# Row maxima and row sums of an attention stage moved through DRAM, and score banks seeded by ScalarE in every step

## What is computed

```python
xn = group_norm(x, gn_gamma, gn_beta)
qkv = jnp.einsum('bchw,oc->bohw', xn, w_qkv).reshape(B, 3, nh, d, H * W)   # nh = 4, d = 64
q, k, v = (qkv[:, 0], qkv[:, 1], qkv[:, 2])
scores = jnp.einsum('bhci,bhcj->bhij', q, k) * d ** (-0.5)
attn = jax.nn.softmax(scores, axis=-1)
out = jnp.einsum('bhij,bhcj->bhci', attn, v).reshape(B, C, H, W)
proj = jnp.einsum('bchw,oc->bohw', out, w_proj) + b_proj[None, :, None, None]
return xn + proj
```

## Time and profile before

| what | value |
|---|---|
| median of 3 runs | 5492.59 us (5486.8 to 5498.76) |
| the profiled execution | 5486.11 us |
| its span, from first to last instruction | 5484.3 us |
| PE busy in the span | 4957.6 us (90%) |
| DVE busy | 3959.3 us (72%) |
| POOL busy | 2966.1 us (54%) |
| ACT busy | 2793.4 us (51%) |
| granted PE clock, mean | 0.959 of full speed |

### The profile page before, as it was taken

The page is one execution under the profiler, slowest core; times in us unless marked ns, Lnnn a source line. Parts: engine busy times, 40 slices in busy tenths (PEclk is TensorE's granted clock), DMA queues, the critical chain, the costliest instruction groups (busy, mean ns, idle before and its releaser), DMA issues. The chain is left out here.

```text
span 5484.3 us, 73719 instructions
## 1 busy us (share of the span) xinstructions
PE 4957.6 (90%) x22320; PEld 2313.6 (42%) x22320; DVE 3959.3 (72%) x6354; ACT 2793.4 (51%) x4750; POOL 2966.1 (54%) x2339
## 2 busy tenths in 40 slices
PE   7999999999899999999978869969978996999788
PEld 3333333333333333333346657745544553554344
DVE  4788888883588888888333334458887886898898
ACT  2666666664266666666411111135544554555455
POOL 0555555555055555555437757746645664665675
PEclk9999999999999999999978879989999998999899
DMA  2000000000000000000134435569969998998998
GB/s 73 1 1 1 1 1 1 1 1 34 30 1 1 1 1 1 1 1 1 37 87 128 128 111 163 162 242 365 388 268 350 371 389 304 378 387 350 396 410 358
DMA packets 320271, 812.24 MB, mean 148 GB/s; under 512 B 70094, under 2 KB 137556, under 8 KB 319758
## 3 DMA queue, kind: packets, MB, share of 16 engines
q0 software_dynamic: 193536, 679.59, 32.8%
q1 hardware_dynamic: 126478, 129.39, 6.9%
HBM read 708.40 MB, written 100.43 MB: 147 GB/s over the span
## 5 line engine op out<-in xcount | busy, mean ns | idle before, releaser
L653 POOL TENSOR_TENSOR arena<-arena 128x1024 f32<-128x1024 f32 x480 | 1168.0, 2433 | 955.2 <-ACT arena L1310 952.6
L1841 DVE TENSOR_REDUCE arena<-ps 128x2 f32<-128x1024 f32 x1024 | 1252.2, 1223 | 457.5 <-PE ps L805 454.2
L705 POOL DMA_INDIRECT arena<-corners,arena x1152 | 1094.2, 950 | 687.6 <-issue 301.6
L1310 ACT ACTIVATE arena<-ps 128x1024 f32<-128x1024 f32 x1024 | 995.4, 1022 | 611.2 <-PE ps L834 609.4
L2065 DVE SCALAR_TENSOR_TENSOR ps<-arena,ps 128x256 f32<-128x256 f32 x2304 | 956.3, 483 | 230.9 <-DVEq L2059 220.9
L1172 PE MATMUL ps<-arena 128*128 128x512 f32 x2304 | 1047.5, 598 | 0.2
L834 PE MATMUL ps<-arena 64*128 64x512 f32 x4096 | 977.9, 590 | 19.0 <-ACT ps L1293 19.0
L847 PE MATMUL ps<-arena 128*64 128x512 f32 x4096 | 991.3, 605 | 0.0
L1503 ACT ACTIVATE ps<-arena 128x256 f32<-128x256 f32 x1152 | 500.2, 469 | 471.0 <-DMA arena<-corners,arena 208.4
L689 POOL DMA_INDIRECT arena<-corners,arena x576 | 544.8, 946 | 275.5 <-issue 244.3
L1860 DVE TENSOR_TENSOR arena<-arena 128x1024 f32<-128x1024 f32 x480 | 630.5, 1314 | 79.3 <-ACT arena L1310 79.3
(11 more groups left out here) (165 smaller groups left out, 4108.5 us busy)
## 6 DMA issues: line engine op xcount, KB each, us to landing
corners<-arena SPq DMA_DIRECT2D x256, 256.0 KB
arena<-corners,arena POOLq DMA_INDIRECT x1728, 7.7
img<-in_x SPq DMA_DIRECT2D x8, 1024.0 KB, 9.3
corners<-arena SPq DMA_DIRECT2D x128, 64.0 KB, 2.2
arena<-in_wd SPq DMA_DIRECT2D x2, 2304.0 KB, 8.5
between<-img SPq DMA_DIRECT2D x4, 1024.0 KB, 5.9
arena<-between SPq DMA_DIRECT2D x4, 1024.0 KB, 10.5
resid<-img SPq DMA_DIRECT2D x8, 512.0 KB, 3.4
```

The source lines that it names most:

```text
L653: pool.tensor_tensor(SUMS[u % 2][:, 0], SUMS[u % 2][:, 0], PAIR[g % 2][:, :, 0], ALU.add).then_inc(sum_a, 2)
L705: pool.indirect_dma_start(G3[4 * k + t].rearrange("p a c -> p (a c)"), None, table256[b], bass.IndirectOffsetOnAxis(ap=IS3[:, k, t:t + 1], ...
L1310: af(P[n % 4].rearrange("p h q -> p (h q)"), ps[:, 2 * (n % 2):2 * (n % 2) + 2, :].rearrange("p h q -> p (h q)"), ACT.Exp, scale=float(D) ...
L1841: v.tensor_reduce(mxp[i % 2][:, :, j], ps[:, 4:6, :], AX.X, ALU.max).then_inc(mx_done, 1)
```

## The change

The maxima no longer go through PE and ACT. DVE writes the negated maximum of eight steps to MNEG and scales it into MROWS (f16, two values a partition); SP stores it to `row_buf` in DRAM, and after the fourth store of a block loads the 1024 values to all 128 partitions as MWIDE, now doubled and with the two heads interleaved. ACT seeds the banks of every step but the first two of an image, whose rank-one products take their row from MWIDE. POOL adds the two halves of the row sums together (`fold`), so that PE's row sums take half the products; the sums go through DRAM to be inverted in a [128, 8] tile, and come back widened over the partitions. In the last block the inverse is made as before.

```diff
-        MROW = [att.f32(CHUNK, dt=F16) for _ in range(2)]
-        MWIDE = att.f32(2, CHUNK, dt=F16)
-        MSTAT = att.f32(128)
+        MWIDE = [att.f32(CHUNK, 2, dt=F16) for _ in range(2)]
+        MNEG = att.f32(2)
+        MROWS = [att.f32(4, 2, dt=F16) for _ in range(2)]
+        SINV = att.f32(2, 4)
...
+        def is_seeded(n):
+            return n >= 2
...
+                def send_row(u, t):
+                    sp.wait_ge(mrow_ready, 4 * u + t + 1)
+                    if u >= 2:
+                        sp.wait_ge(wide_ready, 16 * (u - 1))
+                    sp.dma_start(row_buf[u % 2, t * 256:(t + 1) * 256].rearrange("(p h) -> p h", h=2),
+                                 MROWS[u % 2][:, t, :]).then_inc(row_sent, 16)
+                def spread_rows(u):
+                    sp.wait_ge(row_sent, 64 * (u + 1))
+                    if u >= 2:
+                        sp.wait_ge(p_ready, NT * (u - 1))
+                    sp.dma_start(MWIDE[u % 2].rearrange("p q h -> p (q h)"),
+                                 row_buf[u % 2, :].partition_broadcast(128)).then_inc(wide_ready, 16)
+                def send_sums(u):
+                    sp.wait_ge(sums_copied, u + 1)
+                    for h in range(2):
+                        sp.dma_start(sum_buf[h:h + 1, :], RC[64 * h:64 * h + 1, :]).then_inc(sums_sent, 16)
+                    sp.wait_ge(sums_sent, 32 * (u + 1))
+                    sp.dma_start(SINV, sum_buf.rearrange("h (p i) -> p h i", p=128)).then_inc(sums_back, 16)
+                def spread_inverses(u):
+                    sp.wait_ge(rc_done, u + 1)
...
+                    sp.dma_start(inv_buf.rearrange("h (p i) -> p h i", p=128), SINV).then_inc(inv_sent, 16)
+                    sp.wait_ge(inv_sent, 16 * (u + 1))
+                    for h in range(2):
+                        sp.dma_start(RC[64 * h:64 * h + 64, :],
+                                     inv_buf[h, :].partition_broadcast(64)).then_inc(rc_wide, 16)
+                for u in range(BLOCKS + 1):
+                    if u < BLOCKS:
+                        send_row(u, 0)
+                    if u >= 2:
+                        send_sums(u - 2)
+                    if u < BLOCKS:
+                        send_row(u, 1)
+                    if u >= 2:
+                        spread_inverses(u - 2)
+                    if u < BLOCKS:
+                        send_row(u, 2)
+                        send_row(u, 3)
+                        spread_rows(u)
...
+                def fold(u):
+                    pool.wait_ge(sum_a, NT * (u + 1))
+                    pool.wait_ge(sum_b, NT * (u + 1))
+                    for h in range(2):
+                        to = SUMS[u % 2][:, h]
+                        pool.tensor_tensor(to[:, 0], to[:, 0], to[:, 1], ALU.add).then_inc(folded, 1)
...
+                    if pair == 0 and u >= 1:
+                        fold(u - 1)
...
-                    if n % 2 == 0 or n == 1:
+                    if is_seeded(n):
+                        pe.wait_ge(seeded, seeds_before[n] + 1)
+                    else:
                         for h in range(2):
                             rows = slice(64 * h, 64 * h + 64)
-                            mm(ps[:, 2 * (n % 2) + h, :], COEF[rows, :], MROW[u % 2][rows, :], start=True, stop=False,
+                            mm(ps[:, 2 * (n % 2) + h, :], COEF[rows, :], MWIDE[u % 2][rows, :, h], start=True, stop=False,
                                tile_position=(64 * h, 0))
-                    else:
-                        pe.wait_ge(seeded, n // 2)
...
-                    for part in range(2):
-                        for h in range(2):
-                            last = mm(ps[64 * h:64 * h + 64, 7, :], ONES, SUMS[u % 2][:, h, part, :], start=(part == 0),
-                                      stop=(part == 1), tile_position=(0, 64 * h))
+                    for h in range(2):
+                        last = mm(ps[64 * h:64 * h + 64, 7, :], ONES, SUMS[u % 2][:, h, 0, :], start=True, stop=True,
+                                  tile_position=(0, 64 * h))
...
                 def seed(n):
-                    act.wait_ge(aux_done, aux_at[("wide1", n // NT)] + 1)
+                    act.wait_ge(wide_ready, 16 * (n // NT + 1))
                     act.wait_ge(p_ready, n - 1)
-                    af(ps[:, 2:4, :].rearrange("p h q -> p (h q)"), MWIDE.rearrange("p h q -> p (h q)"), ACT.Copy,
-                       scale=ROW_COEF).then_inc(seeded, 1)
+                    bank = 2 * (n % 2)
+                    af(ps[:, bank:bank + 2, :], MWIDE[n // NT % 2].rearrange("p q h -> p h q"), ACT.Copy, scale=ROW_COEF).then_inc(seeded, 1)
...
                     weights(2 * g)
                     weights(2 * g + 1)
...
+                    for n in (2 * g + 2, 2 * g + 3):
+                        if n < STEPS and is_seeded(n):
+                            seed(n)
...
+                    v.tensor_reduce(MNEG, mxp[i % 2], AX.X, ALU.max, negate=True).then_inc(mneg_ready, 1)
+                    dve.wait_ge(mneg_ready, i + 1)
...
+                    v.tensor_scalar(MROWS[i // 4 % 2][:, i % 4, :], MNEG, 1.0 / (HALF_SCALE ** 2 * ROW_COEF), None,
+                                    ALU.mult).then_inc(mrow_ready, 1)
...
-                    if g >= NT // 2 and 3 <= g % (NT // 2) <= 10:
-                        inverse_sums(g // (NT // 2) - 1, g % (NT // 2) - 3)
+                    if g >= NT // 2 and g % (NT // 2) == 6:
+                        inverse_sums(g // (NT // 2) - 1)
```

More of the change, by code:

```diff
@@ L299, in program @@
                 opening.append(("max", i))
[L300 to L305, removed]
         def sums_in(g):
             return g // (NT // 2) - 1 if g >= NT // 2 and g % (NT // 2) == 2 else None
[L310 to L326, removed]
+        def is_seeded(n):
+            return n >= 2
+        seeds_before = [sum(is_seeded(m) for m in range(n)) for n in range(STEPS + 1)]
         block = ctx.enter_context(nc.Block())
@@ L608, in _ @@
                 inverse_root(grs[:, :])
-                for what, value in ((COEF, 0.0), (MSTAT, 0.0), (ONES, 1.0)):
+                for what, value in ((COEF, 0.0), (ONES, 1.0)):
                     pool.memset(what, value).then_inc(pool_step, 1)
-                pool.wait_ge(pool_step, 3)
-                pool.sem_inc(pool_step, -3)
+                pool.wait_ge(pool_step, 2)
+                pool.sem_inc(pool_step, -2)
                 for h in range(2):
@@ L658, in _ @@
                         normalized(u - 1)
+                fold(BLOCKS - 1)
                 normalized(BLOCKS - 1)
@@ L874, in _ @@
                         unit(i)
-                    elif what == "max":
+                    else:
                         leading_scores(i)
-                    else:
-                        max_rows(i)
-                for h in range(2):
-                    wide_rows(0, h)
                 pe.wait_ge(unit_copied, len(units))
@@ L1335, in _ @@
                         unit_copy(i)
-                    elif what == "rows":
-                        row_copy(i)
-                for h in range(2):
-                    wide_copy(0, h)
                 for g in range(STEPS // 2):
@@ L1342, in _ @@
                     weights(2 * g + 1)
-                    if wide_in(g) is not None:
-                        for h in range(2):
-                            act.wait_ge(seeded, g)
-                            wide_copy(wide_in(g), h)
-                    if seeds_in(g) is not None:
-                        seed(seeds_in(g))
-                    if rows_in(g) is not None:
-                        row_copy(rows_in(g))
+                    for n in (2 * g + 2, 2 * g + 3):
+                        if n < STEPS and is_seeded(n):
+                            seed(n)
                     if sums_in(g) is not None:
```

104 lines of the change are left out of this document (53 added, 51 removed).

## The result

The changed kernel takes **5625.4 us** (5619.8 to 5632.6, four runs) against 5489.7 for the kernel before on the same chip: a ratio of 1.0246 [1.0227, 1.0265], 136 us slower where 5366 us and a gain were forecast. The profiled execution took 5627.5 us, its span 5625.7, and the mean granted clock fell from 0.959 to 0.941.

A forecast was written before the change was run, and what follows sets the result against it. PE was taken to set the pace at 4.34 us a pair, ACT afterwards at 4.20. Terms summed to 63.3 us an image, twice 126.6, off 5486.1, plus 6.5 for the median: 5366 us, range 5335 to 5400 (8 in 10: 5310 to 5430).

The forecast's parts named there:

- cost the transfers at nothing: Chain from a block's last maximum to its first seed: transfers of 4.7 to 6.3 us, hidden in 7.1.
- the maxima come late: Rival, first seed of each block: transfers queue or need 2 us more, PE stands; 5402 to 5426 us; chance 0.12.
- slower seeds: Rival, both seeds of each pair: reading every second f16 value is slower; 5671 us at 1.33 us a seed; chance 0.08.
- Part 2: Transposes leave PE, 15.0 us gained an image; the new DVE scaling in four pairs has over 0.1 us to spare.
- ACT closes the round at 4.20: In ordinary pairs of steps, ACT's two exponentials and two seeds set the pace at 4.20 us, above PE's 4.13.
- The sign that I had named: In ordinary pairs of 4.15 to 4.25 us, PE's idle time would be put down to ACT's seed.
- The rival with PE as the bound at 4.13: Rival, each pair: seeds overlap better, PE sets the pace at 4.13 us; 5316 to 5330 us; chance 0.15.
- the one in which the pair stays at 4.34: Rival, each pair: the rounds of PE, ACT, DVE and POOL disturb each other; about 5440 us; chance 0.05.
- Part 1: Rank-one products leave PE: 237 pairs go from 4.34 to 4.20 us, 33.2 us gained an image.
- Part 6: POOL against DVE, each block: collisions cost 2.1 us against 1.0 before, 0.5 of it the fold; 16 lost an image.
- SP's queue: Sums and inverses sent between row stores have three or four pairs, over 12 us; returned sums are back by pair 5.
- Parts 3, 4, 5 and 7: Row sums 19.8 us gained an image, wide rows 19.5 gained, `raw_output` 3.0 lost; ends 5.1 and 1.6 lost, 1.5 gained.

The follow-up runs named there:

- e5_noscale40: The changed kernel with the leading scores 40 steps ahead instead of 36 and no scaling of the maxima on DVE: 5365.3 us, 0.9766.
- the control: The kernel before the change with the leading scores 40 steps ahead and everything else in its place: 5500.5 us, 1.0012.
- lead 40: The changed kernel with the leading scores 40 steps ahead instead of 36, nothing else: 5423.0 us, 0.9877.
- e6_odd_noscale40: The kernel of e5_noscale40 with ACT seeding only the odd steps, even steps taking the rank-one product: 5408.0 us, 0.9849.
- lead 34: The changed kernel with the leading scores 34 steps ahead instead of 36: 5749.6 us, 1.0469.
- e2_odd: The changed kernel with ACT seeding only the odd steps, even steps taking the rank-one product from MWIDE: 5608.4 us, 1.0213.

## Why the prediction was wrong

**The failed step is the one that cost the transfers at nothing.** It put the store at 3.5 us, by the row with the same bytes, and the load at 2.8; they took 7.6 and 4.7. The chain is 12.3 us where I had 4.7 to 6.3 at the outside, in a window of 7.1. Both ends of my range came from transfers of another shape: the 3.5 us are those of `bnf` (L408 of the kernel before), 64 pieces of 8 bytes from one SBUF tile to another, the 1.9 us a load, and none of them writes to DRAM. I matched bytes, and what makes this store dear is that it is 128 pieces of 4 bytes lying side by side (7.2 us in L451, against 2.9 in L453 and 1.5 in L459). With 12.3 + 1.1 for the DVE operations against 7.1 + 0.5, the seed is 5.8 us late, and PE's wait shows 5.89 in the block above, 5.6 in the mean (167.4 / 30). The rival "the maxima come late" was the right one. Its price, 30 us for each us, was 29.6 from lead 36 to 34; for the first 5.8 us it was some 35, as it left out the slow clock behind the wait. Its size, 1.2 to 2 us, was a third of the truth or less. It had 0.12, and I let it end at 5426. The case that I put above the time before, slower seeds, did not occur (1.025 us).

**A second term of the sum was mis-sized.** Part 2 called the scaling "one tiny operation" with 0.1 us to spare. Alone it is 0.17 us; its median is 1.03. The prediction asked of DVE's adds and of its copy what POOL does to them, and not of this operation, which ends with POOL's add all the same (521.55 above). Its removal is worth 57.7 us with the chain covered, 84.7 without.

With both put right the time is 5365.3 us (5625.4 less 202.4 for the longer lead less 57.7 for the scaling), and I had forecast 5366. So these two make up the miss as a whole. That the last digit agrees is luck: parts erred both ways, and the runs stand on different chips. A block of `e5_noscale40` takes 69.4 us (507.37 to 576.81 between two copies of the row sums), 1.0 less than the 70.4 of the prediction. Against it, its first scores start 5.7 us later (146.6 for 140.9), as the opening is longer (145.3 in the control), and 12 us more lie behind the last scores, in work that the change leaves alone (2817.7 for 2805.5; the control has 2812.8, so part of it is only the run).

The other steps, by the runs in which nothing is late:
- *ACT closes the round at 4.20.* Right. With lead 40:

```profile
552.57 0.39 PE L871 MATMUL ps<-arena 64*128 64x512 f16 x2
552.79 1.96 PE L892 MATMUL ps<-arena 64*128 64x512 f32 x8
...
556.77 0.39 PE L871 MATMUL ps<-arena 64*128 64x512 f16 x2
```

  that is 4.20 us, and the scores in it take 1.96 where they took 1.88. The sign that I had named, idle time of PE put down to the seed in ordinary pairs, is hardly there: nearly all of the 9.8 us in 38 waits lie in the last pairs of an image. There the leading scores are gone and PE's own work was 3.90 us a pair, so the round shows by itself. In `e5_noscale40`:

```profile
1224.60 2.07 PE L891 MATMUL ps<-arena 64*128 64x512 f32 x8 [0.26 <-ACT ps L1321]
...
1228.80 2.07 PE L891 MATMUL ps<-arena 64*128 64x512 f32 x8 [0.26 <-ACT ps L1321]
```

  The pair takes 4.20 with PE waiting for a seed in each. The rival with PE as the bound at 4.13 is out, as is the one in which the pair stays at 4.34.
- *Part 1* gave 33.2 us an image, 66 in all, for the rank-one products; `e6_odd_noscale40` shows 42.7. But that run also has fewer waits for DVE, 28.0 us for 45.1; with those 17 added the rank-one products alone would be worth about 60, an estimate from the two runs.
- *Part 6*, collisions with POOL: 2.1 us a block, 61 in all, against 45.1 us of PE's waits for DVE. But 12.0 of these lie in the two openings; in the blocks it is 32.9 us, 20.4 in the kernel before, where I had put 61 and 29. By the waits that the profile records it is about half of my figure. I had weighed the rule of GPSIMD Engine Reference (Specifications) in the Trainium skill, that POOL shares its SBUF interfaces with a DVE operation in a 2-port mode. The trace agrees: DVE's copy took 0.68 us before; now it meets the fold in nearly every block. That it runs in this mode no row shows. Its durations, and one meeting:

```profile
L1877 DVE COPY arena<-arena x32: 682/1670/1680, 145.7 to 2750.3; 128x1024 f32<-128x1024 f32 x32
```
```profile
537.18 1.67 DVE L1877 COPY arena<-arena 128x1024 f32<-128x1024 f32 x1
```
```profile
535.81 2.50 POOL L698 TENSOR_TENSOR arena<-arena 128x512 f32<-128x512 f32 x2
```

  1.0 us lost a block: between my 0.5 and the 1.2 by the rule, and nearer to the rule. That is DVE's time; what the copy alone costs PE was not tried.
- *SP's queue* was as forecast where the chain is covered: the returned sums are in time, and no wait for them shows among PE's. What I had not seen is that a transfer behind a slow one inherits its lateness: the store to `inv_buf` takes 5.6 us in the changed kernel and 9.0 with lead 34, where it is issued 4.6 and 0.5 us behind a row store (at 479.56 and 484.13; at 502.15 and 502.60), and 1.8 with lead 40, where 11.6 us lie between them (523.16 and 534.77).
- Parts 3, 4, 5 and 7 were not tried one by one. Some can be read in `e5_noscale40`: with row sums, values start to leading scores is now 2.72 us (504.53 to 507.25), 1.34 less than before, for 1.32 in part 3; in part 7 the last pairs take 4.20 as forecast, and the last row sums wait 3.6 us for POOL where they waited 1.1, so 2.5 more, the two folds. Parts 4 and 5 are only held by the block of 69.4 us as a sum.

## What to carry to other kernels

Size a small transfer by its pieces and where they land, not by its bytes: a row of the same bytes in another shape is no bound, and a hand-over that every block waits for should be given its own measured chain and a margin in time. Ask of every small operation on DVE what POOL does at that moment, for a scaling of two elements can wait nearly as long as an add of a thousand (2.1 and 2.3 us). Where a transfer is late, first pack it (here one store of 16 bytes a partition did as much as two pairs of lead), and only then start it earlier.

## What the runs showed of the hardware that I had not expected

- 128 pieces of 4 bytes packed in DRAM take 7.2 us to land, of 8 bytes 2.9, of 16 bytes 2.0, of 64 bytes 1.5; 4-byte pieces 64 bytes apart take 2.9 (medians of ten each, one run).
- A two-element scaling on DVE takes 0.17 us, or up to 2.1 beside POOL. The reduction just before it, with the same two results, stays at 0.17, also inside POOL's add (521.34 above).
- ACT copies 1024 f16 values with a step of 4 bytes as fast as neighbouring ones (1.025 us, before 1.028), and takes 2.035 with a step of 16, in the one pattern tried.
- The granted clock fell to 0.75 in the stretch with the 5.89 us wait and to 0.67 in the 5 us behind it, between the 1.2 and the 2.4 GHz levels on average, and was 1.00 again from 535 on; the first scores after it took 3.63 us for 1.88. Such a late transfer is paid about 1.3 times: per block 5.9 us of waiting and some 1.7 us of slow matmuls. With the 3.43 us wait of `e2_odd` it stayed at 1.00.
